# The per-key constant of the scores in three cross-attention sublayers: from a VectorE add to a one-row matmul that accumulates in PSUM

## The reference, cut to what matters

```python
q = x @ Wq + bq                      # L1: x goes through one more linear layer first
k = ctx @ Wk + bk ; v = ctx @ Wv + bv
scores = q @ k.T / sqrt(256)         # 77 scores per token; L3 alone: where(mask == 0, -1e9, scores)
x = layernorm(x + softmax(scores) @ v @ Wo + bo)
```

## Time and profile before

| | |
|---|---|
| median of 3 runs | 3376.15 us (3374.84 to 3385.19) |
| the profiled execution: its time, its span | 3376.15 us, 3374.3 us |
| mean granted TensorE clock over the span | 0.873 of full speed |
| TensorE matmul / weight load busy | 2615.7 us (78%) / 1689.0 us (50%) |
| VectorE / ScalarE / GpSimd busy | 1739.6 us (52%) / 858.2 us (25%) / 383.6 us (11%) |
| L1_xattn, L2_xattn, L3_xattn | from 1012.9, 2005.4 and 3096.9 us, some 50 to 62 us each |

### The profile page before, as it was taken

One profiled execution on the slowest core, in us unless ns is written; L12 is line 12 of the kernel. 1 busy time (PEld: TensorE's weight loads), 2 busy tenths in 40 slices (PEclk: granted clock), 3 DMA queues, 4 the chain that ended last, 5 costly groups with the idle time before them and its releaser, 6 DMA issues. The chain is left out here.

```text
span 3374.3 us, 36270 instructions
## 1 busy us (share of the span) xinstructions
PE 2615.7 (78%) x14146; PEld 1689.0 (50%) x14146; DVE 1739.6 (52%) x2603; ACT 858.2 (25%) x1168; POOL 383.6 (11%) x263
## 2 busy tenths in 40 slices
PE   6877856478888599669999885259994999998444
PEld 4665633222247488346656644236671676764221
DVE  8996754487743211345555545711104554553776
ACT  1113564235541132133323310001110221221111
POOL 3321301400010200100000000030003010100000
PEclk8988978779997699789999995569996999999677
DMA  3004000534300355132212100023212100000000
GB/s 92 1 1 150 2 0 25 118 54 66 53 21 1 119 194 196 32 95 80 80 54 80 53 10 1 21 98 121 89 50 68 39 14 11 19 5 24 26 0 25
DMA packets 79655, 184.71 MB, mean 55 GB/s; under 512 B 15512, under 2 KB 47011, under 8 KB 75796
## 3 DMA queue, kind: packets, MB, share of 16 engines
q1 hardware_dynamic: 72756, 136.83, 14.4%
q0 software_dynamic: 6768, 46.07, 3.7%
HBM read 148.99 MB, written 33.69 MB: 54 GB/s over the span
## 5 line engine op out<-in xcount | busy, mean ns | idle before, releaser
L1690 PE MATMUL L_ffn_h_ps<-L_ffn_xgT,L_ffn_w 128*128 128x512 f32 (+1 forms) x992 | 250.4, 413 | 1.2 <-DVE L_ffn_xgT L1733 1.2
L1702 PE MATMUL L_ffn_y_ps<-L_ffn_w,L_ffn_h 128*128 128x256 f32 x1120 | 247.2, 381 | 3.8 <-ACT L_ffn_h L1720 2.9
L1720 ACT ACTIVATE L_ffn_h<-L_ffn_h_ps,L_ffn_w 128x256 f32<-128x256 f32 (+1 forms) x184 | 107.6, 585 | 542.5 <-PE L_ffn_h_ps L1690 542.5
L2285 PE MATMUL L_attn_X<-xT,L_attn_w 128*128 128x512 f32 x512 | 228.7, 600 | 11.9 <-DMA L_attn_w<-in_L_attn_w 11.9
L1702 PEld LDWEIGHTS L_ffn_y_ps<-L_ffn_w,L_ffn_h 128*128 128x128 f32 x1120 | 210.9, 190 | 35.4 <-ACT L_ffn_h L1720 4.6
L600 DVE TENSOR_REDUCE L_attn_neg<-L_attn_R 128x1 f32<-128x512 f32 (+3 forms) x304 | 187.4, 657 | 54.9 <-PE L_attn_R L477 53.4
L1690 PEld LDWEIGHTS L_ffn_h_ps<-L_ffn_xgT,L_ffn_w 128*128 128x128 f32 x992 | 167.7, 193 | 82.2 <-issue 64.3
L477 PE MATMUL L_attn_R<-L_attn_K,L_attn_Q 104*128 104x512 bf16 (+3 forms) x384 | 119.6, 363 | 82.7 <-DVE L_attn_K L594 48.6
L1733 DVE COPY L_ffn_xgT<-L_ffn_t_ps 128x256 f32<-128x256 f32 x70 | 27.1, 420 | 280.4 <-PE L_ffn_t_ps L1677 280.4
L566 ACT ACTIVATE L_attn_probs<-L_attn_S 128x1024 f32<-128x1024 f32 (+1 forms) x192 | 147.3, 812 | 79.5 <-PE L_attn_S L523 78.8
L2285 PEld LDWEIGHTS L_attn_X<-xT,L_attn_w 128*128 128x128 f32 x512 | 95.5, 192 | 122.3 <-issue 120.5
(11 more groups left out here) (511 smaller groups left out, 4997.8 us busy)
## 6 DMA issues: line engine op xcount, KB each, us to landing
L_ffn_w<-in_L_ffn_w SPq DMA_DIRECT2D x8, 2180.0 KB, 9.6
L_attn_bc<-decays SPq DMA_DIRECT2D x32, 512.0 KB, 7.0
L_attn_w<-in_L_attn_w SPq DMA_DIRECT2D x16, 640.0 KB, 4.0
L_attn_bp<-decays SPq DMA_DIRECT2D x32, 256.0 KB, 7.2
L_attn_Q<-L_attn_q_parts SPq DMA_DIRECT2D x48, 128.0 KB, 5.2
L_attn_K<-L_attn_k_parts SPq DMA_DIRECT2D x48, 128.0 KB, 8.2
L_attn_w<-in_L_attn_w SPq DMA_DIRECT2D x16, 384.0 KB, 3.0
slot_tokens<-zero SPq DMA_DIRECT2D x1, 5120.0 KB, 24.9
```

Of the source, the lines that this page charges most:

```text
L1690: ins = nc.tensor.matmul(h_ps[f % 2][:, lo // CW, 0:hi - lo], w1[u][:, kt, f * P:(f + 1) * P], xgT[u][:, kt, lo:hi], start=kt == 0, stop=k ...
L1702: ins = nc.tensor.matmul(y_ps[(u * tiles + s) % 2][:], h[:, f, s * P:(s + 1) * P], w2[u][:, f, :], start=f == 0, stop=f == FT - 1)
L1720: nc.scalar.activation(h[:, f, :], h_ps[f % 2][:].rearrange("p c n -> p (c n)")[:, 0:S], func, bias=b1[u][:, f:f + 1]).then_inc(sem["act_d ...
L2285: ins = nc.tensor.matmul(x[:, c * CW:(c + 1) * CW], w[1 - par][:, kt, r, :], xT[:, kt, b * T + c * CW:b * T + (c + 1) * CW], start=kt == 0 ...
```

## The change

`s_const` is kept on one partition, and a third matmul per tile adds it inside PSUM: its weights are a row of 128 ones, its moving operand is the 77 numbers. The VectorE add of `s_const` goes away. In L3 the add of the mask stays, and what goes away there is the preparation that put `s_const` into `fill` (L3154). The matmul that computes `s_const` has one column of weights instead of 128. VectorE sets the row of ones at its start and TensorE waits for it once. In L1 and L2 the bank is now free for the group after next when `centred` is signalled, not `filled`. In L1 and L2 the maximum and the subtraction read PSUM instead of SBUF.

```diff
+        one_row = m.sb("one_row", [1, P])
-        s_const = m.sb("s_const", [P, CK])
+        s_const = m.sb("s_const", [1, CK])
...
-                        mm = nc.tensor.matmul(s_ps[0][:, 0:CK], col[:, kt:kt + 1].broadcast_to([P, P]), src[:, kt, :],
+                        mm = nc.tensor.matmul(s_ps[0][0:1, 0:CK], col[:, kt:kt + 1], src[:, kt, :],
...
             def scores(g):
                 if g >= 2:
-                    pe.wait_ge(filled, g - 1)
+                    pe.wait_ge(filled if masked else centred, g - 1)
...
-                        mm = nc.tensor.matmul(dst, xT[:, kt, n * P:(n + 1) * P], kq[:, kt, b * S2:(b + 1) * S2], start=kt == 0, stop=kt == KT - 1)
+                        nc.tensor.matmul(dst, xT[:, kt, n * P:(n + 1) * P], kq[:, kt, b * S2:(b + 1) * S2], start=kt == 0, stop=False)
+                    mm = nc.tensor.matmul(dst, one_row[:], s_const[:, b * S2:(b + 1) * S2], start=False, stop=True)
                 mm.then_inc(s_mm, 1)
...
+            pe.wait_ge(one_set, 1)
             pe.wait_ge(kq_ready, 2)
...
-            nc.scalar.copy(s_const[:], s_ps[0][:, 0:CK]).then_inc(kq_ready, 1)
+            nc.scalar.copy(s_const[:], s_ps[0][0:1, 0:CK]).then_inc(kq_ready, 1)
...
+            nc.vector.memset(one_row[:], 1.0).then_inc(one_set, 1)
...
-            dve.wait_ge(kq_ready, 2)
             if masked:
                 dve.wait_ge(fill_set, 1)
-                for b in range(B):
-                    tiles = slice(b * TT, (b + 1) * TT)
-                    last = nc.vector.tensor_tensor(fill[:, tiles, :], fill[:, tiles, :], over(s_const[:, b * S2:(b + 1) * S2], TT), ALU.add)
-                last.then_inc(fill_set, 1)
-                dve.wait_ge(fill_set, 2)
...
-                bias = fill[:, n, :] if masked else over(s_const[:, b * S2:(b + 1) * S2], SUB)
-                nc.vector.tensor_tensor(s[g][:], src, bias, ALU.add).then_inc(filled, 1)
-                dve.wait_ge(filled, g + 1)
-                src = s[g][:]
+                if masked:
+                    nc.vector.tensor_tensor(s[g][:], src, fill[:, n, :], ALU.add).then_inc(filled, 1)
+                    dve.wait_ge(filled, g + 1)
+                    src = s[g][:]
```

More of the change, by code:

```diff
@@ L2938, in context_stage @@
         x_back, x_back_read = m.sem("x_back"), m.sem("x_back_read")
-        (ctx_mm, ctx_ready, const_ready, k_mm, k_ready, v_mm, v_ready, a1_mm, a1_ready, k1_mm, k1_ready, kq_mm,
+        (one_set, ctx_mm, ctx_ready, const_ready, k_mm, k_ready, v_mm, v_ready, a1_mm, a1_ready, k1_mm, k1_ready, kq_mm,
          kq_ready, vo_mm, vo_ready, wx_mm, wx_ready, keep_set, fill_set, s_mm, filled, max_done, centred, exp_done, den_done, den_inv, p_ready,
          p_turned, pT_ready) = [m.sem(n) for n in (
-             "ctx_mm", "ctx_ready", "const_ready", "k_mm", "k_ready", "v_mm", "v_ready", "a1_mm", "a1_ready", "k1_mm",
+             "one_set", "ctx_mm", "ctx_ready", "const_ready", "k_mm", "k_ready", "v_mm", "v_ready", "a1_mm", "a1_ready", "k1_mm",
              "k1_ready", "kq_mm", "kq_ready", "vo_mm", "vo_ready", "wx_mm", "wx_ready", "keep_set", "fill_set", "s_mm", "filled", "max_done",
@@ L3160, in centre @@
                 src = s_ps[g % 2][:, 0:SUB * S2].rearrange("p (t k) -> p t k", k=S2)
-                b = g * SUB // TT
                 dve.wait_ge(s_mm, g + 1)
-                bias = fill[:, n, :] if masked else over(s_const[:, b * S2:(b + 1) * S2], SUB)
-                nc.vector.tensor_tensor(s[g][:], src, bias, ALU.add).then_inc(filled, 1)
-                dve.wait_ge(filled, g + 1)
-                src = s[g][:]
+                if masked:
+                    nc.vector.tensor_tensor(s[g][:], src, fill[:, n, :], ALU.add).then_inc(filled, 1)
+                    dve.wait_ge(filled, g + 1)
+                    src = s[g][:]
                 nc.vector.tensor_reduce(mx[:, n], src, X_AXIS, ALU.max).then_inc(max_done, 1)
```

## The result

The changed kernel takes 3426.6 us (median of 4 runs, 3422.71 to 3433.16) against 3377.79 us for the kernel before beside it (4 runs, 3374.84 to 3385.19). The ratio is 1.0147, 95% interval 1.0128 to 1.0168: slower by 1.5%, some 49 us, where 18 were forecast. The direction was right; the time lies outside the range. The profiled execution took 3425.38 us, its span is 3423.5 us, and the mean clock fell from 0.873 to 0.864.

The account below looks back on a forecast made before the run. No engine saturated; each stage's timeline of TensorE and VectorE waits decides. L2 5.2 + L3 5.2 + L1 7.3 + constants 0.6 = 18.3 us on 3376.15 gives 3394.5 us; likeliest case 3388 to 3400, wider range 3380 to 3405.

Parts of the forecast that it names:

- The group of scores: Four tiles' score matmuls on TensorE: from 1.9 to 4.0 us, 2.1 us more (0.9 to 2.5).
- The switch: Change between 128-row and one-row loads in the scores: 0.16 us each (0 to 0.20), 8 per group, 1.3 us.
- Where it lands: Longer score groups carried through each stage's waits: L2 +5.2 us, L3 +5.2 us, L1 +7.3 us.
- the list of waits: TensorE and VectorE waits around `turn(0)` and `scores(3)`, less idle time and cover: +5.2 in L2 and L3, +7.3 in L1.
- the records-only rival: Scores in L1 to L3: one-row matmuls cost only their records, 0.9 us a group; about +5.5 us, 3381.5; chance 0.13.
- VectorE (adds gone, PSUM as a source): L1 to L3: dropped operations give back at most 5.6 us; maximum and subtraction from PSUM in L1, L2 cost nothing.
- The constants: Computing `s_const` with one column: possible switches in and out, 0.2 us per stage, 0.6 in all.
- The clock: Rival, scores: half clock for one or two groups, +4 to +10 us on top, some 3402; chance 0.11.
- That witness: L0_xattn, cited against the falling clock: runs with such switches all the time at 0.98 over 72 us.
- The test that the prediction set itself: Score groups in the profile after: far more than 4.4 us would mean the clock or a dearer drain.

Follow-up runs that it names:

- the extra matmuls: Changed kernel plus two more matmuls per tile (128 rows, 154 columns) into columns of the bank nobody reads: 3422.66 us, ratio 1.0142.
- the kernel without the switch: Changed kernel with 128 rows of weights of 1/128 in the third matmul and the constant on 128 partitions: 3382.18 us, ratio 1.0024.
- the grouped form: Changed kernel with the four one-row matmuls of a group behind its 16 other records, 2 switches a group: 3390.13 us, ratio 1.005.

## Why the prediction was wrong

**The group of scores (+2.1 us): right, at full clock.** 3.93 against 4.0 us. The switch was sized at 0.16 and measured 0.15; that 77 rows are no switch was read rightly from the earlier trace rows.

**Where it lands (+5.2, +5.2, +7.3): right as far as the runs can tell.** At full clock the list of waits isn't seen alone in the changed kernel. Its rule holds where the clock is kept: 13.2 worked out and 13.6 measured in L2 with the extra matmuls, 13.5 and 13.8 in L3. For the kernel without the switch, the sums of the records-only rival (1.0 for L2, 5.5 us in all) stand against 1.04 us in the window of L2 and 5.6 us in the median. For L1 no run shows it at full clock. One slip is in it: for `turn(0)` of L3 it takes 3.8 us a group where its own sum gives 4.0, which makes that stage 0.4 us too cheap.

**VectorE (adds gone, PSUM as a source): right.** 479 and 478 ns. **The constants (+0.6 us in all): low,** 0.36 us in L2 and, from the last matmul pair of the values to the first score matmul, 3.70 against 3.39 us in L1, instead of 0.2 each; inside the bounds, and small beside the rest.

**The clock: the step that failed.** It was left out of the sum at a chance of 0.11, and it cost some 32 us by the subtraction below. The prediction named this rival, gave it 0.11 and a price of "+4 to +10 on top", and rejected it because "L0_xattn runs with such switches all the time at 0.98 over 72 us". That witness is wrong. In that window of the kernel before, the one-row line is this:

```profile
L1038 PE MATMUL L_xattn_x_ps<-L_xattn_ob,L_xattn_one_row x18: 374/426/478, 326.7 to 388.5; 1*128 1x256 f32 x18
```

That is nine pairs in 62 us, one in about 7 us; the new order has one in 0.97 us. "Such switches all the time" took their presence for their density. Other loads there come after a pause as well, those of 32 rows and those behind the 32-column ones; from one one-row load to the next, 6.88 us:

```profile
326.67 0.29 PEld L1038 LDWEIGHTS L_xattn_x_ps<-L_xattn_ob,L_xattn_one_row 1*128 1x128 f32 x2 [0.33 <-issue]
327.29 0.87 PEld L1016 LDWEIGHTS L_xattn_t_ps<-ident,L_xattn_s 128*77 128x77 f32 x8 [0.33 <-issue]
328.32 0.57 PEld L1007 LDWEIGHTS L_xattn_S_ps<-L_xattn_kz,L_xattn_qT 32*128 32x128 f32 x16 [0.16 <-issue]
329.75 0.81 PEld L1027 LDWEIGHTS L_xattn_q_ps<-L_xattn_pT,L_xattn_v 77*32 77x32 f32 x32 [0.86 <-ACT L_xattn_pT L1091]
330.76 0.87 PEld L1016 LDWEIGHTS L_xattn_t_ps<-ident,L_xattn_s 128*77 128x77 f32 x8 [0.20 <-issue]
```

With them it is five changes of shape in 6.88 us against two in 0.97, a third of the density. But their pauses are longer: 0.33 + 0.16 + 0.20 and another 0.33 ahead of the next one-row load make 1.02 us of 6.88, without the wait for ScalarE; that is 15% of the time, and 0.16 of 0.97 is 16%. So the loader's idle share doesn't tell the two stages apart either. What also differs is the width of the matmuls: 128 to 256 columns there, 77 in the scores, and 154 in the extra matmuls that kept the clock up. Which of this counts was not tried.

The prediction also looked at the clock in L1 alone, and read it as the effect of a long wait. The clock fell there at 1035.6, when the wait had lasted 2.0 of its 2.70 us. And L2 of the kernel before already had 13.5 us at half clock, from 2035.7 on, where the waits ahead of the fall were short, 1.31 us the longest (timeline rows, then the row of the window at half clock):

```profile
2031.67 0.66 PE L3039 MATMUL L_xattn_t_ps<-ident,L_xattn_s 128*77 128x128 f32 x4 [1.31 <-ACT L_xattn_s L3106]
2032.78 1.10 PE L3051 MATMUL L_xattn_y_ps<-L_xattn_v,L_xattn_pT 77*128 77x256 f32 x4 [0.45 <-DVE x_tok L2794]
...
2035.70:2049.20 13.50, 9.42 (x33) 7.09 (x32) 10.15 (x34) 3.32 (x6) 3.10 (x4) 0.50 0.00 0
```

The price was too low as well, and by the number of groups, not by the size of one. A group at half clock takes 6.70 - 3.93 = 2.8 us more, inside the "1.9 to 3 us" of the prediction. It assumed "one or two groups", but in L2 the clock fell 4.0 us after the first score matmul and stayed down for 30.7 us, so that three groups of four, the transposes and values between them and part of the tail ran at 1.2 GHz; in L3 it stayed down for 44.4 us, in L1 for 20.5. By subtraction: L1 16.35 - 7.3 = 9.1, L2 16.77 - 5.2 = 11.6, L3 17.07 - 5.2 = 11.9, together some 32 of the 50 us. The experiments bear out the subtraction for L2 and L3: where the extra matmuls keep the clock up, the same 8 switches per group cost what the list says and no more. For L1 it stays an estimate.

The test that the prediction set itself ("if a group takes far more than 4.4, the clock or a dearer drain is at work") told where to look: the groups of 6.7 us stand in the stretches at 0.50, and the first group of L2, at 1.00, takes 3.93. A dearer drain at full clock is excluded.

The Trainium skill has the shape of this in "TensorE: Matmul & The Clock Gate", section "A second HAM failure mode: psum-queue depth-cycling": an engine that pauses briefly and often between its matmuls can have its clock go back and forth. The trace agrees that no long wait is needed: in L2 TensorE waits for nobody in the 4.0 us before the fall, and is counted busy for all of 30.72 us at 0.50. It differs in that the pauses there are those of switches and not waits for PSUM, and in that the clock stayed down for these 30.72 us on end.

What stays open is why the switches bring the clock down. That the change of shape does it is shown; that the time without work does it is only argued. Neither the number of switches nor that of records sorts the kernels: 8 switches per group hold the clock in L2 and L3 with two extra matmuls a tile and not with one, and 2 switches per group hold it there in the grouped form (3390 us), but only in some stages with one wide one-row matmul. That the moment at which a stage begins decides in such cases would fit the runs of 3387 to 3412 us of one kernel, but was not tried.

## What to carry to other kernels

A matmul with one row between matmuls with 128 isn't a cheap bias: here a tile took 0.97 us instead of 0.67, and then the clock fell for much of what stood around it. Where a constant must go through TensorE, give it as many rows as its neighbours have (1/128 in 128 rows) and do it once per bank; this version was level with the kernel before. Before moving work to TensorE to relieve another engine, leave that work out altogether and time it: here the ceiling was 2.4 us of 3376 by the windows, too little to show in the median. And when a stage is taken as a witness for the clock, it isn't enough that the same kind of pause occurs in it: compare how often the pauses come and how wide the matmuls between them are, and doubt the witness where either differs.

## What was not expected of the hardware

- TensorE's clock fell to 0.50 in L2 with no wait for another engine in the 4.0 us ahead of the fall, and stayed there with TensorE busy for 30.72 us of 30.72.
- Adding 64 records to L2 made it 3.2 us shorter (51.90 against 55.09 us in L2), with the clock at 0.84 instead of 0.60; in L1, where the clock fell all the same, the stage grew by 3.8 us.
- The same share of idle loader, 15% and 16%, went with a clock of 0.98 in L0_xattn and with its fall in the new scores.
- A change between 64 and 128 rows costs what one between one and 128 rows does: tiles of 0.97 us in both.
- One column instead of 128 in the constant is a switch too: the loader is idle for 0.37 us before its loads and 0.27 after them, 0.26 to 0.36 us more in L2, though each load takes only 82 ns.
